# Layer 4 of a gated cross-attention stack: the next unit's scores issued ahead of the current unit's values

## The reference

```
x = x + tanh(g_xattn[3]) * L3_xattn(layernorm(x), ctx, Wq, Wk, Wv, Wo)
x = x + tanh(g_ffn[3])   * L3_ffn(layernorm(x), ...)
```

```
q = (latents @ Wq) per head;  k, v = (concat(context, latents) @ Wk, Wv) per group
attn = softmax(q k^T / sqrt(128));  out = (attn v, heads side by side) @ Wo
```

## Time and profile before

| | |
|---|---|
| time, median of 3 runs | 2787.57 us (2781.22 to 2788.70) |
| the profiled execution | 2788.8 us |
| its span (first to last instruction) | 2786.9 us |
| TensorE (PE) busy | 97% of the span, 14736 matmuls |
| VectorE, ScalarE, GpSimd busy | 64%, 40%, 30% |
| mean granted TensorE clock | 0.988 of full speed |

### The profile page before, as it was taken

The page is one execution under the profiler, slowest core; times in us unless marked ns, Lnnn a source line. Parts: engine busy times, 40 slices in busy tenths (PEclk is TensorE's granted clock), DMA queues, the critical chain, the costliest instruction groups (busy, mean ns, idle before and its releaser), DMA issues.

```text
span 2786.9 us, 45264 instructions
## 1 busy us (share of the span) xinstructions
PE 2692.4 (97%) x14736; PEld 2269.1 (81%) x14736; DVE 1778.8 (64%) x3503; ACT 1114.9 (40%) x3080; POOL 827.4 (30%) x707
## 2 busy tenths in 40 slices
PE   6997999999999999899999999999999999999998
PEld 5885788888888887777888888778878888888887
DVE  5756646446446446677998999845453666666667
ACT  3541333333333333125666666521123444444442
POOL 4002334324324324143232323245533222222210
PEclk9998999999999999999999999999999999999999
DMA  5001111101101101011111111112211110001000
GB/s 148 16 5 63 38 31 54 38 26 53 41 23 53 45 23 50 27 44 38 35 30 34 30 34 31 30 47 56 57 46 42 31 27 28 28 27 31 28 5 31
DMA packets 59789, 106.01 MB, mean 38 GB/s; under 512 B 7184, under 2 KB 11536, under 8 KB 59536
## 3 DMA queue, kind: packets, MB, share of 16 engines
q1 hardware_dynamic: 56448, 96.49, 12.4%
q10 hardware_dynamic: 3216, 7.81, 0.8%
HBM read 100.09 MB, written 2.10 MB: 37 GB/s over the span
## 4 chain that ended last, share of the span: by engine, by line
PE 92%; DVE 5%; ACT 1%; issue 1%; POOL 1%; DMA 0%; ACTq 0%; DVEq 0%; POOLq 0%
PE four L629 51%; PE outp L629 25%; PE value L629 9%; PE turned L987 4%; PE turned L751 1%; DVE stats L1648 1%; PE turned L676 0%; DVE x L1909 0%; DVE xt_lo L1677 0%; PE value L676 0%; DMA raw<-in_stream 0%; DVE probs L1672 0%; DVE x L2121 0%; PE turned L629 0%; POOL w_lo L604 0%
## 5 line engine op out<-in xcount | busy, mean ns | idle before, releaser
L600 POOL TENSOR_TENSOR w_hi<-raw,zero 128x512 fp32r<-128x512 f32 x347 | 371.5, 1071 | 1811.7 <-PE four L629 619.7
L1909 DVE SCALAR_TENSOR_TENSOR x<-outp,g_inv,x 128x512 f32<-128x512 f32 x768 | 548.5, 747 | 337.1 <-PE outp L629 336.5
L604 POOL TENSOR_TENSOR w_lo<-raw,w_hi 128x512 fp32r<-128x512 f32 x352 | 454.3, 1291 | 31.5 <-ACT w_hi L1268 4.3
L629 PE MATMUL four<-xt_hi,w_lo 128*128 128x512 f32 x1024 | 429.7, 420 | 5.4 <-DVE xt_lo L1677 4.7
L629 PE MATMUL four<-xt_hi,w_hi 128*128 128x512 f32 x1024 | 404.8, 395 | 0.0
L629 PE MATMUL four<-xt_lo,w_hi 128*128 128x512 f32 x1024 | 403.4, 394 | 0.0
L629 PE MATMUL outp<-w_hi,a_lo 128*128 128x512 f32 x800 | 327.7, 410 | 17.1 <-DVE a_lo L2008 7.6
L629 PE MATMUL outp<-w_hi,a_hi 128*128 128x512 f32 x800 | 317.2, 396 | 0.0
L629 PE MATMUL outp<-w_lo,a_hi 128*128 128x512 f32 x800 | 317.0, 396 | 0.0
L1475 ACT ACTIVATE probs<-probs,top 128x128 f32<-128x128 f32 x512 | 199.6, 391 | 211.5 <-DVE top L1953 126.3
L1268 ACT ACTIVATE pT<-turned 128x512 f32<-128x512 f32 x320 | 192.4, 601 | 203.5 <-PE turned L987 145.6
(11 more groups left out here) (285 smaller groups left out, 4900.1 us busy)
## 6 DMA issues: line engine op xcount, KB each, us to landing
raw<-in_stream SPq DMA_DIRECT2D x352, 256.0 KB, 2.6
ctx_raw<-in_ctx_t ACTq DMA_DIRECT2D x4, 512.0 KB, 6.2
x<-in_x_in ACTq DMA_DIRECT2D x2, 1024.0 KB, 10.7
kz<-kT SPq DMA_DIRECT2D x32, 64.0 KB, 2.7
pb<-in_position_bias ACTq DMA_DIRECT2D x1, 2048.0 KB, 8.1
out<-x SPq DMA_DIRECT2D x8, 256.0 KB, 2.0
qw<-in_qweight ACTq DMA_DIRECT2D x1, 768.0 KB, 3.9
ln_w<-in_ln_weight ACTq DMA_DIRECT2D x1, 256.0 KB, 2.8
```

Of the source, the lines that this page charges most:

```text
L600: pool.tensor_tensor(w_hi[:, k, :], raw[:, k % RAW, :], zero[:, :].to_broadcast([P, D]), ALU.add)\
L604: pool.tensor_tensor(w_lo[:, k, :], raw[:, k % RAW, :], f32(w_hi[:, k, :]), ALU.subtract)\
L629: m = pe.matmul(out_, l, r, start=start, stop=stop, skip_group_check=True)
L1909: dve.scalar_tensor_tensor(out=x[:, b, :], in0=O[no_f(k) % 2][:, :], scalar=scale, in1=x[:, b, :], op0=ALU.mult, op1=ALU.add)\
```

## The change

In layer 4 alone, TensorE's `step(k)` no longer begins with `scores(k)`. Instead `scores(k+1)` is issued in step k, behind `output(k-2)` and ahead of `values(k-1)`. The first unit's scores stay where they were. The order on TensorE in a step becomes `turn(k-1)`, query part, `output(k-2)`, `scores(k+1)`, `values(k-1)`, and the next step's `turn(k)` follows the values directly. Nothing else changes: the same instructions, the same waits, the same buffers, and the other engines' programs as they were.

```diff
         KEY_LAG = 3
+        SCORES_FIRST = (3,)
         DENSE_AHEAD = 6
...
                 def step(k, it):
-                    if k < L.NU:
+                    if k < L.NU and (k == 0 or n not in SCORES_FIRST):
                         scores(k, it)
...
                     if L.has_O(k) and not (n in (1, 2) and (L.parts(k) or n == 2 and L.sums_head(k))):
                         output(k - L.lag_o, it)
+                    if k + 1 < L.NU and n in SCORES_FIRST:
+                        scores(k + 1, it)
                     if L.has_V(k):
                         values(k - L.lag_v, it)
```

## The result

| | before | after |
|---|---|---|
| median time | 2785.89 us (20 runs, 2781.22 to 2792.67) | 2791.17 us (20 runs, 2786.75 to 2795.26) |
| ratio after to before | | 1.0017, 95% interval 1.0010 to 1.0024 |
| profiled execution, its span | 2788.8, 2786.9 us | 2790.4, 2788.6 us |
| layer 4's attention, first scores to last output (starts in the timeline) | 615.36 us | 620.26 us |

The changed kernel is slower by 0.17%, some 4.7 us (the medians lie 5.3 apart). That lies inside the 0.3% which the prediction called "the same", but the whole interval is above 1. The attention of layer 4 alone grew by 4.90 us between the two traces, enough for the whole difference. The two profiled spans are only 1.7 apart, because the trace after reaches this attention 3.8 earlier (2129.34 against 2133.14); the change touches nothing ahead of it. So what follows goes by lengths within the attention.

A forecast was written before the change was run, and what follows sets the result against it. TensorE was taken to bound the kernel. Borders -1.3, last units' scores +2.8 and late keys +1.9 made +3.4 us; from a three-run median of 2787.57 the forecast was 2791.0 us, range 2784 to 2797.

The forecast's parts named there:

- What bounds the kernel: Layer 4: TensorE makes 92% of the chain, is busy throughout at full clock, and waits 1.9 us, at the ends.
- What a border costs: Float32 to split on TensorE: nothing by load starts, which it took; 0.08 us per border by recorded durations.
- The term itself, -1.3 us: Borders in layer 4's units: 0.01 us net gain in each of 126 units, ends -2.5 and +2.5.
- The scores of the last units, +2.8 us: Units 124 to 127: scores no longer run inside output's wait for `a_lo`; 4 x 0.71 us.
- The late keys, +1.9 us: Changes of key group: earlier scores wait for DVE's key splits, 6 x 0.32 us, ends 0 and 3.8.
- the 0.26: Time from `a_lo`'s end to output's start in the last units, added to `k_lo`'s 4.18 to give 4.44.
- The sign named for it: TensorE's list of waits should show scores waiting for `k_lo` some six times at 0.3 us.
- The spare 0.53 us of the full units: Full units, values to output: of 1.24 us spare, 0.71 goes and 0.53 stays, so no wait for `a_lo`.
- rival (b): Output waits for `a_lo` in every unit; 0.1 us beyond the spare time gives about 2803 us; chance 0.06.

The follow-up runs named there:

- e3: Kernel before, with each full unit's float32 work cut into four stretches instead of two; ratio 1.0009, interval 1.0000 to 1.0019.
- e5: As e3, but values and scores whole in the last units, as in the kernel before; ratio 1.0000 to the kernel before.
- e1: Changed kernel with the scores of units 124 to 127 back at the start of their own step; ratio 1.0014 to the kernel before.
- e6: Kernel before with the change applied only to the scores of units 124 to 127; 2787.36 us in one run, attention 618.21 us.
- e2: As e1, and the keys of a new group split one step earlier; ratio 1.0002 to the kernel before.
- e4: Changed kernel with output ahead of the query part in every unit; 2898.82 us in one run, 107.7 above the changed kernel's median.

## Why the prediction was right

The forecast was 2791.0 us and the measured median 2791.17. That nearness is luck, since two misses cancel: the base that the forecast stood on, three runs, was 1.7 us above the median of twenty, and the difference was forecast too small. It was +3.4 us, the measured one 4.7 us (2.8 to 6.7 by the interval of the ratio), and 4.90 in the attention. What holds is the direction, and the two terms that lengthen the time, by place and nearly by size. Against the 4.90 the sum is low by 1.5: 2.1 too low in the border term, 0.6 to 0.8 too high in the keys.

- **What bounds the kernel**: right. TensorE's share of the chain and its clock did not change, and 4.1 of the 4.9 us lie at waits of TensorE and at their cover.
- **What a border costs**: the decision between two readings was right, and it carried the case. The starts of the weight loads tell the pace; the long first record doesn't. e3 doubled the borders and no unit grew. The rule of the Trainium skill that stood beside it (Perfetto Trace Analysis, section "Tensor Engine Instruction (MATMUL, LD_WEIGHTS)") is a start taken at the prefetch and an end computed from the instruction's size. The start agrees with the earlier trace rows: the long record begins 0.02 behind its own load and ends on the pace, 0.13 before the next (2308.58 and 2308.71). The computed end cannot be the recorded start plus a fixed time, since two matmuls of one size are recorded 0.36 and 0.28 long.
- **The term itself, -1.3 us**, had the wrong sign: a unit is 0.007 us longer, +0.8 us, inside the ends that were given (-2.5 and +2.5). A hitch of 0.01 still stands behind the scores, now ahead of the values. But that the 0.007 is owed to the border is not shown: e3 and e5, with one order, differ by 0.017 a unit, more than what was to be explained. Why units of one order differ by a hundredth of a us stays open.
- **The scores of the last units, +2.8 us**: right, 2.96 measured, and 2.82 and 2.85 by e1 and e6. The price was read from one row, the place from the order of the work. The waits of output for `a_lo` came four times more than before, at 0.69 to 0.86 each, where the prediction said some 0.9.
- **The late keys, +1.9 us**: right in place and number, six waits in units where a query half precedes, but mis-sized. They cost 1.1 us by the table and 1.27 by e2. The step that failed is the 0.26 taken from DVE's end to TensorE's start at the other wait; here it was 0.06 to the load and 0.11 for it. The sign named for it, scores in the list of TensorE's waits, did not come either: the wait shows only at the weight loads.
- **The spare 0.53 us of the full units**: right. Output starts 2.72 after values and 2.19 would do, and e4 shows the same 2.18 in full units. So rival (b) did not happen, and its price of 12 us for each 0.1 beyond was about right: by its expectation e4 was 0.86 beyond, and it cost 108.

## What to carry to other kernels

A matmul whose record is longer than its neighbours need not have cost more (0.36 at a border cost nothing; 0.47 behind the wait of e4 went with 0.08 lost): compare the starts of the weight loads, and price a border between two kinds of work by the pace across it. When a piece of work is moved, look at what it was covering in the units that are not like the rest, the first, the last, and those at a change of group; a steady unit with spare time says nothing on them. A wait on a weight load is not in the list of the matmuls' waits; read the PEld groups too.

## What the runs showed of the hardware that was not expected

The time from DVE's recorded end to TensorE's start differs between waits: 0.06 us at the keys (2284.55 to 2284.61, load and matmul record alike), but 0.24 at `a_lo` (2728.74 to 2728.98 in the chain of the last units, the row called issue, which ends with the output's first record). In the trace after the change all six waits for keys show the first, and five of the six at `a_lo` the second. The two places differ in the waits that stand there; which of these makes the difference was not tried.

The mean length of a full unit is steady to a thousandth between kernels of one order (4.833 before and in e6, 4.840 after and in e1 and e2), but e3 and e5 differ by 0.017 us with the same instructions per unit. The 0.017 is not at one border: by the mean starts over 45 full units of each, no piece has more than 0.007 of it (the first query half). It took two kernels of one order to see that a hundredth of a us per unit was not evidence.
